# Two-layer attention block on one core: O normalised inside the attention, one row-sum group per chunk, and other tiles for the adding DMAs

## The reference

```python
# layer 0, for each image; 8 heads of 32 channels, n = 4096
q, k, v = split(einsum('oc,bchw->bohw', w_qkv, x), 3)
scores = einsum('bhdi,bhdj->bhij', q, k) / sqrt(32)
attn = softmax(scores, axis=-1)
out = einsum('bhij,bhdj->bhdi', attn, v)
x1 = einsum('oc,bchw->bohw', w_proj, out) + x
# layer 1: non-local block with 2x2 max pooling of g and phi, one head
f = einsum('bnc,bcm->bnm', theta(x1[:, :64]), maxpool(phi(x1[:, 64:])))
y = einsum('bnm,bmc->bnc', softmax(f), maxpool(g(x1)))
result = batchnorm(W(y)) + x1
```

## Time and profile before

| | before |
|---|---|
| median of the runs | 2471.96 us |
| the profiled execution: own time / span | 2472.93 us / 2471.2 us |
| PE busy | 2412.8 us (98%) |
| ACT busy | 2213.5 us (90%) |
| DVE busy | 2136.4 us (86%) |
| POOL busy | 456.8 us (18%) |
| mean granted TensorE clock | 0.996 |

### The profile page before, as it was taken

The page is one execution under the profiler, slowest core; times in us unless marked ns, Lnnn a source line. Parts: engine busy times, 40 slices in busy tenths (PEclk is TensorE's granted clock), DMA queues, the critical chain, the costliest instruction groups (busy, mean ns, idle before and its releaser), DMA issues.

```text
span 2471.2 us, 79834 instructions
## 1 busy us (share of the span) xinstructions
PE 2412.8 (98%) x35892; PEld 1143.7 (46%) x35892; DVE 2136.4 (86%) x1338; ACT 2213.5 (90%) x1842; POOL 456.8 (18%) x652
## 2 busy tenths in 40 slices
PE   8999999999999999999999999999999999998997
PEld 4444444444444444344454444444544444443443
DVE  6999999969999999895579999999799999997854
ACT  7999999989999999576489999999899999994763
POOL 0222222202222222010012222222022222220200
PEclk9999999999999999999999999999999999999999
DMA  8877878767777777502277877777678777773011
GB/s 243 166 159 161 162 159 164 152 181 163 161 158 162 162 161 155 151 1 78 80 203 162 164 160 162 160 160 149 185 161 165 157 163 162 159 158 119 1 65 40
DMA packets 150279, 360.34 MB, mean 146 GB/s; under 512 B 23088, under 2 KB 65392, under 8 KB 149680
## 3 DMA queue, kind: packets, MB, share of 16 engines
q0 software_dynamic: 73728, 268.47, 54.4%
q1 hardware_dynamic: 76208, 86.78, 11.4%
HBM read 52.63 MB, written 33.85 MB: 35 GB/s over the span
## 4 chain that ended last, share of the span: by engine, by line
PE 85%; ACT 6%; DVE 3%; SPq 2%; DMA 2%; issue 1%; POOL 0%; ACTq 0%; DVEq 0%; POOLq 0%
PE scores L526 33%; PE psOL L539 33%; PE psOL L961 7%; ACT arena L606 5%; PE scores L347 3%; DVE arena L655 2%; PE psOL L885 1%; PE scores L358 1%; PE psOL L502 1%; PE scores L948 1%; PE scores L949 1%; PE psOL L510 1%; PE scores L938 1%; SPq L1249 1%; PE scores L939 1%
## 5 line engine op out<-in xcount | busy, mean ns | idle before, releaser
L606 ACT ACTIVATE arena<-scores 128x1536 f32<-128x1536 f32 x1368 | 1835.9, 1550 | 0.5
L655 DVE TENSOR_TENSOR arena<-arena 128x2048 f32<-128x2048 f32 x732 | 1674.8, 2291 | 106.0 <-ACT arena L606 52.0
L526 PE MATMUL scores<-arena 96*32 96x512 f16 x16384 | 1125.6, 379 | 8.1 <-ACT arena L606 8.0
L539 PE MATMUL psOL<-arena 128*32 128x256 f32 (+3 forms) x15968 | 1110.3, 384 | 0.5
L526 PEld LDWEIGHTS scores<-arena 96*32 96x32 f16 x16384 | 383.2, 95 | 604.0 <-ACT arena L606 399.5
L539 PEld LDWEIGHTS psOL<-arena 128*32 128x32 f32 x15968 | 471.2, 110 | 355.4 <-issue 27.7
L684 POOL DMA_DIRECT2D arena<-arena x448 | 388.6, 895 | 1121.2 <-ACT arena L606 831.5
L961 PE MATMUL psOL<-arena 128*128 128x512 f16 x768 | 171.9, 381 | 0.0
L681 POOL DMA_DIRECT2D arena<-arena x64 | 35.3, 556 | 558.2 <-ACT arena L606 557.9
L1226 DVE SCALAR_TENSOR_TENSOR arena<-arena 128x1536 f16<-128x1536 f32 (+1 forms) x48 | 75.8, 1580 | 70.0 <-ACT arena L1078 63.9
L1071 ACT ACTIVATE arena<-scores 128x1536 f32<-128x1536 f32 (+1 forms) x48 | 62.5, 1302 | 75.7 <-PE scores L949 75.7
(11 more groups left out here) (119 smaller groups left out, 1159.4 us busy)
## 6 DMA issues: line engine op xcount, KB each, us to landing
arena<-arena POOLq DMA_DIRECT2D x512, 512.0 KB, 5.4
arena<-qk_parts SPq DMA_DIRECT2D x192, 128.0 KB, 3.8
qk_parts<-arena SPq DMA_DIRECT2D x32, 512.0 KB, 3.7
X<-in_x SPq DMA_DIRECT2D x16, 512.0 KB, 5.1
att_out<-arena SPq DMA_DIRECT2D x32, 256.0 KB, 3.4
arena<-att_out SPq DMA_DIRECT2D x16, 512.0 KB, 10.6
out<-arena SPq DMA_DIRECT2D x32, 256.0 KB, 2.0
arena<-att_inv SPq DMA_DIRECT2D x16, 256.0 KB
```

Source lines behind the costliest of these rows:

```text
L526: last = nc.tensor.matmul(bank[k % 2][m * D:(m + 1) * D, i * CH:(i + 1) * CH], KS[0:3 * D, h, j * 128 + m * D:j * 128 + (m + 1) * D], QS2[ ...
L539: last = nc.tensor.matmul(both(c)[h * D:(h + 1) * D, lo:hi], V[:, j, h * D:(h + 1) * D], P[:, r + h, lo:hi], start=(j == 0 and lo == 0), s ...
L606: nc.scalar.activation(P[:, u % RING:u % RING + size, :], bank[k % 2][:, 0:size * CH].rearrange("p (u n) -> p u n", n=CH), ACT.Exp, scale= ...
L655: nc.vector.tensor_tensor(new, old, P[:, r:r + G, :], ALU.add).then_inc(s_add, 1)
```

## The change

- SUM_D becomes 4, 7, 11, 14, 17, 21, 24, 27; VectorE has 24 tiles as before, the others.
- For chunks 0 to 6 accD is added to acc by a pair of adding DMAs (one for each half, 512 KB) that GpSimd issues after the chunk's last tile, and TensorE makes one group of ones-matmuls instead of two, 12 steps after the chunk's end (`sums_of_merged`). Chunk 7 keeps three groups (`sums_of_last`). QUARTERS is worked out for this.
- The sums are copied at addition 9 and the reciprocal taken at addition 13. SyncE stores the reciprocal, waits for the store, and loads it spread over 32 partitions per head into L (four DMAs of 64 KB). GpSimd multiplies Ost by L (a 128x512 float32 product, semaphore s_even) after it has issued the DMAs of tile 21 of the next chunk, and then SyncE stores the normalised output. This is done for chunks 0 to 6.
- The second layer drops seven of the eight `normalise` instructions, the `broadcast` of chunks 0 to 2 and the eight spread loads; only chunk 7 is normalised there. Its loads are otherwise the same; chunks 1, 2 and 3 are now loaded at the last score group.

```diff
-SUM_D = [2, 6, 9, 13, 16, 20, 23, 27]
+SUM_D = [4, 7, 11, 14, 17, 21, 24, 27]
...
+SUMS, BEHIND = 12, 4
+SUM_STEPS = [exps_through(c, JT - 1) + SUMS for c in range(NC - 1)]
...
-    rate = 4 * (JT + 2) * GROUP / (G * JT)
+    rate = 4 * (JT + 1) * GROUP / (G * JT)
...
+            def sums_of_merged(pe, c):
+                pe.wait_ge(s_o_free, c + 1)
+                for k in range(2):
+                    pe.wait_ge(s_merge[k], 16 * (c + 1))
                 for h in range(G):
+                    last = nc.tensor.matmul(both(c)[h * D:(h + 1) * D, :], ones[:], acc[c % 2][:, h, :],
+                                            start=True, stop=True)
                 last.then_inc(s_sum, 1)
...
-                        if n == 12 and c:
+                        if n == 9 and c:
                             sums_out(dve, c - 1)
...
-                        if n == 16 and c:
+                        if n == 13 and c:
                             dve.wait_ge(s_out, 16 * c)
                             nc.vector.reciprocal(Ls[:, g, c - 1:c, :], Ls[:, g, c - 1:c, :]).then_inc(s_inv, 1)
...
+                        if c and i == len(SUM_D) - 3:
+                            pool.wait_ge(s_o_free, c)
+                            pool.wait_ge(s_spread, 16 * G * c)
+                            nc.gpsimd.tensor_tensor(Ost, Ost, L[:], ALU.mult).then_inc(s_even, 1)
+                    if c < NC - 1:
+                        pool.wait_ge(s_add, adds_by(c))
+                        for k in range(2):
+                            hs = slice(2 * k, 2 * k + 2)
+                            pool.wait_ge(s_dma[k], 16 * len(SUM_D) * (c + 1))
+                            nc.gpsimd.dma_start(acc[c % 2][:, hs, :].rearrange("p h n -> p (h n)"),
+                                                accD[c % 2][:, hs, :].rearrange("p h n -> p (h n)"),
+                                                accum_op=ALU.add).then_inc(s_merge[k], 16)
...
+                        sp.wait_ge(s_r, 16 * (c + 1))
+                        for h in range(G):
+                            sp.dma_start(L[h * D:(h + 1) * D, :], r_dram[b, g * G + h:g * G + h + 1, cs]
+                                         .broadcast_to([D, CH])).then_inc(s_spread, 16)
+                        if c == NC - 2 and early:
+                            early(sp)
+                        sp.wait_ge(s_even, c + 1)
+                        sp.dma_start(o_dram[g, :, cs], Ost).then_inc(s_ost, 16)
...
-                for n in BUFFERS:
-                    spread_rows(sp, dram, n)
-                    c = BY_DMA[n]
-                    if c >= 4:
-                        sp.wait_ge(s_oin[c % 4], 16)
+                for c in range(4, NC - 1):
+                    sp.wait_ge(s_oin[c % 4], 16)
                     output_in(sp, c)
```

More of the change, by code:

```diff
@@ L82 @@
 QUARTERS = quarters_by_step()
-BY_DMA = [3, 4, 5, 6]
-BY_PE = [c for c in range(NC) if c not in BY_DMA]
-BUFFERS = range(4)
 SIDES = [("g", c, k) for c in range(NC) for k in range(CT)] + [("gt", m, 0) for m in range(MT)]
@@ L462, in attention @@
             s_dma = [sem(root, f"s_dma{k}_{g}") for k in range(2)]
+            s_merge = [sem(root, f"s_merge{k}_{g}") for k in range(2)]
             s_ready = sem(root, f"s_ready_{g}")
@@ L835, in tensor, with broadcast @@
             def tensor(pe, b, between):
[L836 to L842 removed]
+                def broadcast():
+                    if between:
                         pe.wait_ge(behind.signals["l_free"], NC)
+                    pe.wait_ge(s_rc, 16 * NG)
                     for g in range(NG):
                         rows = slice(32 * g, 32 * g + G)
[L846 to L847 removed]
+                        last = nc.tensor.matmul(psOL[:, g * CH:(g + 1) * CH], spread[rows, :],
+                                                Rr_last[rows, :], start=True, stop=True)
                     last.then_inc(s_bc, 1)
@@ L1029, in scalar @@
                     scalar_deviation(act)
+                if b is not None:
+                    act.wait_ge(behind.signals["sum"], NC)
                 for c in range(NC + 1):
@@ L1192, in vector @@
                         residual(CT * c)
+                    if c == 0 and between:
+                        between(dve)
                     if c >= 2:
```

156 lines of the change are left out of this document (56 added, 100 removed).

## The result

The changed kernel takes 2577.88 us (median of 4 runs, 2571.34 to 2582.3) against 2475.18 us for the kernel before on the same chip. The ratio is 1.0423 with a 95% interval of 1.0406 to 1.044. One of the four runs of the kernel before took 2820.72 us; the ratio leaves it out, the median of 2475.18 us doesn't. The forecast was 2453 us, with a range of 2438 to 2505. The kernel is slower, by more than the range allowed.

A forecast was written before the change was run, and what follows sets the result against it. ScalarE's exponentials were taken to bound the attention, where all four parts cost or gain 0; the second layer's start gains 8.9 and 10.9 us: 2472.93 - 8.9 - 10.9 = 2453.1, stated as 2453 us, range 2438 to 2505.

The forecast's parts named there:

- What bounds the attention: Four attention stages: ScalarE's exponentials set the step of 1.342 us, 1836 us in all; TensorE is merely matched to it.
- Rival 3: Attention: TensorE sets the pace, so the removed ones-matmuls gain 28 us there too, 2425 us; chance 5%.
- (1): Attention: one group of ones-matmuls fewer in 28 chunks, 28 us of TensorE, hidden by ScalarE's exponentials; gain 0.
- (2): Attention: two more adding DMAs per chunk, landing 11.6 us after the chunk's end against 16.1 allowed; cost 0.
- (3): Attention: product on GpSimd ahead of tiles 24 and 27, whose DMAs still land about 2 us before ScalarE's need; cost 0.
- Rival 1: Attention: the chain through GpSimd's in-order queue outlasts the ring of nine tiles and stops ScalarE, 2495 us; chance 18%.
- (4): Attention: Ost stored only after the product, landed at about 54 us, wanted after 64; `output_out` and additions don't wait.
- The second layer: Start of second layer: `theta_phi` groups 4.73 us apart, `theta_phi(7)` ending earlier; gain 8.9 us in image 0, 10.9 in image 1.
- Rival 4: Start of second layer: VectorE and ScalarE hold the loop at some 5.5 us a chunk, little gain, 2463 us; chance 10%.
- Rival 2: Attention: same chain as Rival 1, too late in some chunks only, 0.3 us a chunk, 8 us, 2461 us; chance 17%.

## Why the prediction was wrong, point by point

**What bounds the attention: right.** ScalarE sets the pace. Wherever nothing stops it a stage is 459 us again, with seven groups of ones-matmuls fewer (459.09 and 459.08 us in the second and third stage with the product behind tile 27). Rival 3, TensorE's pace, is refuted by the same rows: no stage came below 458.8.

**(1) The removed row-sum group, 0: right**, by the same stages.

**(2) The merges, 0: nearly right.** By themselves they stop nothing: with the product behind tile 27 they run in two stages of 459.1 us, and in all four within 3.3 us of it. Beside a chain that is already late they cost some 16 us, by two runs.

**(3) The product in front of tiles 24 and 27, 0: wrong.** This is the step that failed: its cost was put at 0 and is 104.5 us, of the 129.2 by which the profiled execution lies above the 2453.1 of the sum. The rest is the 8.2 of the projections and the 16.4 by which the gains of the second layer fell short; there it is TensorE that waits for tile 27. The mechanism was on paper, as Rival 1, with the steps at which ScalarE would stop; its price was 2495 and the measured one is 2578. The terms of the sum, for the chunk of the chain above (it starts at 103.85 us), as predicted and as measured:

| term | predicted | measured |
|---|---|---|
| reciprocal | 39.7 | 39.8 |
| its store landed | 44 | 45.4 |
| the four loads landed | 48 to 49 | 50.3 |
| product, length | 1.4 | 2.5 (mean 2.27) |
| product ended | 50 | 53.0 |
| tile 24's halves issued | 50, 51 | 52.9, 53.5 |
| tile 24 landed | 56.5 | 63.4 |
| tile 27 issued | 55.5, 56.5 | 60.7, 63.9 |
| tile 27 landed | 62 | 69.1 |

The program order gave the reciprocal exactly. Then, in this chain, every latency came out longer than I had taken it. From issue to landing the store took 5.4 us where I had 4, the four loads 4.8 where I had 4.5; the product waited for VectorE's lock, a wait that I had put in the upper bound and then dropped; and the largest term is the second half of tile 24. I gave it 5.4 us from its issue, the median of all such DMAs, most of which go out one at a time. Two of 512 KB that go out together share the engines, and the second took 9.87 us, the longest of the 93 such seconds in this trace; their median is 7.2 us (6.6 in the kernel before). Together that is 6.9 us at tile 24's landing against 2.2 of spare, and ScalarE wanted the slot 0.9 us earlier than reckoned (it stops at 161.6, 57.8 us into the chunk): 6.9 - 2.2 + 0.9 = 5.6, the 5.69 of its row.

That is the longest stop, not the usual one. Over all 28 products of this trace the reciprocal's start lies 3.4 us ahead of the loads' issue on average (4.3 predicted), this 6.9 us ahead of the product's start (4.6), the product takes 2.3 (1.4), and tile 24 is down 8.8 us behind its end (6.5). So the store was long enough in the sum; the loads and the landing of tile 24 were mis-sized by 2.3 us each and the product by 0.9. Together it is 21.4 us against 16.8: 4.6 too long, less 2.2 - 0.9 = 1.3 of real spare leaves 3.3, beside the 97.8 / 28 = 3.5 us that ScalarE stands still for each product.

The sentence "GpSimd lets the queue run dry while it waits, so that the loads and tile 24 find idle DMA engines" was half right. Here are some windows of the changed kernel (us, busy of PE, PEld, DVE, ACT, POOL, granted clock, DMA share, GB/s):

```profile
149.00:152.00 3.00, 3.00 (x64) 1.51 (x60) 2.90 (x2) 3.00 (x3) 0.00 (x0) 1.00 1.02 191
152.00:157.00 5.00, 5.00 (x100) 2.41 (x96) 4.28 (x3) 5.00 (x5) 2.72 (x2) 1.00 0.13 23
157.00:160.00 3.00, 3.00 (x56) 1.25 (x52) 2.90 (x2) 3.00 (x3) 1.55 (x2) 1.00 0.83 188
160.00:163.00 3.00, 3.00 (x60) 1.17 (x50) 2.90 (x2) 1.64 (x2) 0.00 (x0) 1.00 1.06 195
```

The queue did run dry, from 152 to 157 us (DMA share 0.13), but only behind tile 21, which kept the engines full while the loads were issued. What ended the wait then let more go than tile 24: both its halves at 156.77 and 157.35, the held store of the output (256 KB) at 156.84, and from 159.88 on three loads of the next queries (128 KB each). With them the DMA engines are full again, and tile 24 lands late. That they lengthen it is read from these rows; no run takes them away one by one.

The price per stop was missing a piece as well: behind a pause of 5.66 us TensorE started again at half its clock (below), and ScalarE waited 1.35 us more for scores. Over the whole kernel 24.3 of ScalarE's 97.8 us are such waits for scores.

**(4) The late store of the output, no wait: right.** No row of VectorE is put down to it.

**The second layer: the steps right, one term mis-sized.** The pace of 4.73 us a chunk came as predicted, against Rival 4. TensorE's timeline of the changed kernel at the start of the second layer, the first two `theta_phi`:

```profile
1079.29 1.94 PE L511 MATMUL psOL<-arena,ones 128*32 128x512 f32 x8 [9.69 <-DMA arena<-arena]
...
1087.87 0.38 PE L875 MATMUL scores<-arena,cw_hi 128*128 128x512 f16 x1
...
1092.60 0.38 PE L875 MATMUL scores<-arena,cw_hi 128*128 128x512 f16 x1
```

1092.60 - 1087.87 = 4.73. But the last sums waited 9.69 us for tile 27, and 6.30 us in image 1. I had allowed one DMA of 8 us from 999.5. Here the second half of tile 24, late from chunk 7's product, took 9.14 us, and that of tile 27 could only follow and took 9.07. So `theta_phi(7)` ends 58.5 us after the last exponential (before 56.2) instead of 8.9 us earlier. In image 1 it gained 3.6 us instead of 10.9. The 8 us were too few even without the late product: with the product on VectorE, and without the spread loads, the last half took 9.4 to 10.8 us beside the three loads of O, and the second layer gave 2.1 to 4.2 us an image. Only where the loads of O come after it (product behind tile 27, or loads held) is the gain of the predicted size.

**The rivals.** Rival 1 happened, three times as far above the forecast (125 us against 42). Rival 2 is what the kernel with the product behind tile 24 shows: stages 8.5 us longer in all, where 8 were written. The chance of 18% for Rival 1 was too low for a chain with 2 us of spare over four latencies, each of which scatters by more than a microsecond (the product 1.3 to 3.4 us, tile 24's second half 7.4 to 9.9).

## What to carry to other kernels

An instruction on an in-order queue costs what stands behind it: count its wait, and the wait inside it, against the due time of every DMA queued behind, at the long end of each latency. When held transfers are released they go out together, so take the landing time of the second of a pair, not the median of single ones. Here one index, the product behind tile 27 instead of tile 21, turned a loss of 4% into a gain of 0.8%.

## What the runs showed of the hardware

- **GpSimd and VectorE exclude each other.** A GpSimd product with SBUF operands doesn't run beside a VectorE addition of two SBUF tensors: 28 narrow products took 0.21 to 2.36 us, all but one ending 73 to 79 ns after an addition's end. The wide ones cost 1.1 to 1.3 us and the wait.
- **Adding DMAs of 512 KB by twos.** In the changed kernel those that went out alone took 5.6 us from issue to landing (median), and the second of two issued within 1.1 us of each other 7.2, at most 9.9. Beside the loads of O one took 10.36 us, and 5.02 with the loads held.
- **TensorE's clock after a pause.** In the 5.66 us in which it waited for ScalarE the granted clock fell from 1.00 to 0.50 (1.2 instead of 2.4 GHz); it was still 0.50 from 170 to 172 us and 1.00 again from 174. A group of twelve score matmuls took 1.47 us, the next 1.31 and the one behind it 0.82. A window, and TensorE's timeline, of the changed kernel:

```profile
170.00:172.00 2.00, 2.00 (x16) 0.50 (x12) 1.85 (x1) 1.57 (x2) 0.86 (x1) 0.50 0.90 168
```

```profile
168.83 1.47 PE L527 MATMUL scores<-arena 96*32 96x512 f16 x12 [5.66 <-ACT arena L604]
...
171.79 1.31 PE L527 MATMUL scores<-arena 96*32 96x512 f16 x12
...
173.58 0.82 PE L527 MATMUL scores<-arena 96*32 96x512 f16 x12
```
